# Conv0 as one pass over 108 contraction rows, with x stacked inside SBUF and relu split straight from PSUM, in an audio tower on one core

## What is computed

```python
x = jnp.pad(x, ((0, 0), (0, 0), (pad, pad)), mode='reflect')
y = jax.lax.conv_general_dilated(x, w, (stride,), 'VALID', ...) + b[None, :, None]
m = jnp.mean(y, axis=1, keepdims=True)
v = jnp.var(y, axis=1, keepdims=True, ddof=1)
h = jax.nn.relu((y - m) * jax.lax.rsqrt(v + EPS) * g[None, :, None] + b_n[None, :, None])
```

## Time and profile before

| | us |
|---|---|
| median of 3 runs | 2319.99 (2319.36 to 2320.64) |
| the profiled execution's own time | 2317.79 |
| its span, first to last instruction | 2316.0 |
| TensorE busy in the span | 2077.2 (90%) |
| VectorE, ScalarE, GpSimd busy | 1682.9, 1470.6, 777.3 |
| mean granted TensorE clock | 0.976 of full |

### The profile page before, as it was taken

The page is one execution under the profiler, slowest core; times in us unless marked ns, Lnnn a source line. Parts: engine busy times, 40 slices in busy tenths (PEclk is TensorE's granted clock), DMA queues, the critical chain, the costliest instruction groups (busy, mean ns, idle before and its releaser), DMA issues. The chain is left out here.

```text
span 2316.0 us, 35857 instructions
## 1 busy us (share of the span) xinstructions
PE 2077.2 (90%) x10589; PEld 1492.2 (64%) x10661; DVE 1682.9 (73%) x3691; ACT 1470.6 (63%) x3736; POOL 777.3 (34%) x1413
## 2 busy tenths in 40 slices
PE   4999999999999977999958888888888888877999
PEld 3788888888888865877735555555555555544554
DVE  4677787787787765566558888888888888864555
ACT  1466656666666643444438888888888888863554
POOL 0111211112112110132256555655556555534100
PEclk9999999999999998999969999999999999997999
DMA  3000000000000000000000000000000000000000
GB/s 111 11 7 7 6 10 6 6 9 6 6 9 6 0 0 1 1 1 1 1 0 1 1 1 1 1 1 1 1 1 1 1 1 1 1 1 3 12 10 14
DMA packets 14447, 15.24 MB, mean 7 GB/s; under 512 B 9995, under 2 KB 10251, under 8 KB 14051
## 3 DMA queue, kind: packets, MB, share of 16 engines
q1 hardware_dynamic: 14307, 13.58, 2.0%
HBM read 11.48 MB, written 2.10 MB: 6 GB/s over the span
## 5 line engine op out<-in xcount | busy, mean ns | idle before, releaser
L1416 ACT ACTIVATE apb<-ps,anb,arq 128x128 f32<-128x128 f32 x1024 | 455.9, 461 | 104.2 <-DVE anb L1290 103.6
L1524 POOL TENSOR_TENSOR apb<-apb,arc 128x512 f32<-128x512 f32 x256 | 266.5, 1041 | 236.5 <-DVE arc L1299 236.5
L1169 PE MATMUL ps<-akT,aqT 128*128 128x256 f32 x1024 | 263.5, 380 | 8.8 <-issue 2.5
L1284 DVE TENSOR_REDUCE amx<-ps 128x4 f32<-128x512 f32 x256 | 175.1, 684 | 97.9 <-PE ps L1169 97.3
L1180 PEld LDWEIGHTS ps<-const,apb 128*128 128x128 f32 x1024 | 112.4, 141 | 178.3 <-issue 106.5
L1416 ACT ACTIVATION_READ_ACCUMULATOR apb<-ps,anb,arq 128x1 f32 x1024 | 211.5, 207 | 0.0
L117 PE MATMUL ps<-h0h,w123h 128*128 128x512 f32 x512 | 207.2, 405 | 3.4 <-POOL h0l L602 1.7
L1169 PEld LDWEIGHTS ps<-akT,aqT 128*128 128x128 f32 x1024 | 196.3, 192 | 21.3
L1518 POOL TENSOR_TENSOR aqr<-at 128x512 f32<-128x512 f32 x128 | 163.4, 1277 | 127.1 <-DVE at L1245 127.1
L119 PE MATMUL ps<-h0h,w123l 128*128 128x512 f32 x512 | 202.8, 396 | 0.0
L1180 PE MATMUL ps<-const,apb 128*128 128x128 f32 x1024 | 162.5, 281 | 44.8 <-POOL apb L1524 43.9
(11 more groups left out here) (303 smaller groups left out, 5317.5 us busy)
## 6 DMA issues: line engine op xcount, KB each, us to landing
x<-in_x SPq DMA_DIRECT2D x32, 176.0 KB
out<-fyo SPq DMA_DIRECT2D x16, 128.0 KB, 1.9
w<-in_w SPq DMA_DIRECT2D x1, 1024.0 KB, 7.8
mw<-in_mw SPq DMA_DIRECT2D x1, 1024.0 KB, 9.6
const<-in_const SPq DMA_DIRECT2D x1, 612.0 KB
wqkv<-in_wqkv SPq DMA_DIRECT2D x1, 576.0 KB, 9.7
fw<-in_fw SPq DMA_DIRECT2D x1, 512.0 KB, 8.3
fsel<-in_fsel SPq DMA_DIRECT2D x1, 512.0 KB, 7.9
```

The lines of the kernel that those rows point to most:

```text
L1169: last = pe.matmul(bank[:, p * 2 * T:(p + 1) * 2 * T], qT[:, i % 2, 2 * k + p, :], kT[:, i // 4 % 2, i % 4, :, :].rearrange("p a s -> p (a ...
L1284: ve.tensor_reduce(mx[:, k, :], ps[:, SB[n % 3], :].rearrange("p (h s) -> p h s", h=4), AX_X, ALU.max).then_inc(S["mx"], 1)
L1416: last = ac.activation(pb[:, i % 2, head, :], ps[:, SB[n % 3], h * T:(h + 1) * T], ACT.Exp, bias=nb[:, k, h:h + 1], scale=rq[:, i % 2, hea ...
L1524: po.tensor_tensor(p, p, rc[:, i % 2, 4 * k:4 * k + 4].unsqueeze(2).to_broadcast([T, 4, T]), ALU.mult).then_inc(S["pn"], 1)
```

## The change

- Conv0's three passes become one matmul. A group now has 12 rows (10 taps, conv bias, normalization bias; the last row is left unscaled, with eps 1). Three groups make a tile of 36 rows, and a tile is stacked three times, 108 rows: x high, x low, x high, against weights high, high, low (`w0s`). The stacks `x0k` are filled for each pair by nine transfers inside SBUF, issued by SyncE, from `x0h` and `x0l`, which now have one place instead of two.
- g0 is folded into the weights, so relu needs no scale and no bias. `relu0` on ScalarE writes `h0h` directly, rounding on the way, and `low0` on VectorE computes max(psum, 0) - h0h from PSUM in one instruction of 128x1024. The cast, the tile `h0f` and the subtraction from SBUF go.
- Conv0 uses one pair of banks for both halves, so each piece waits until `low0` has read the last one (`s_h0l`).
- The wait for conv1 of the pair before stands in `relu0` now, on ScalarE (`s_y`).
- conv1 is issued in two parts. The orders of all engines are new, and all rounds are written out; no loop is left.
- Setup gains one multiplication, a load, a clear of `w0s` and nine transfers inside SBUF that fill it. The loads of x have 96 rows instead of 88.

```diff
-        h0f = sb("h0f", [128, 2, 2, T1])
+        xk = sb("x0k", [3 * SR, 2, TILES, CHUNK], F32R)
...
+                def stack(i):
+                    sp.wait_ge(s_xl, i + 1)
+                    if i == 0:
+                        sp.wait_ge(s_zero, 1)
+                    if i >= 2:
+                        sp.wait_ge(s_c0, 4 * (i - 1))
+                    for j in range(TILES):
+                        rows = slice(j * SR, min((j + 1) * SR, GR))
+                        n = rows.stop - rows.start
+                        for part, x in enumerate((xh, xl, xh)):
+                            sp.dma_start(xk[part * SR:part * SR + n, i % 2, j, :].bitcast(F32), x[rows, :].bitcast(F32)
+                                         ).then_inc(st_x[i % 2], 16)
...
                 def conv0(row, half):
...
+                        m = 4 * i + 2 * row + half
+                        if m >= 1:
+                            pe.wait_ge(s_h0l, m)
+                        if row == 0 and half == 0:
+                            pe.wait_ge(st_x[i % 2], 16 * 3 * TILES * (i // 2 + 1))
+                        for n in range(4):
+                            g = 4 * half + n
+                            last = pe.matmul(ps[:, Y0 + n // 2, (n % 2) * GC:(n % 2 + 1) * GC], w0s[:, g, :],
+                                             xk[:, i % 2, g // PER, row * GC:(row + 1) * GC], start=True, stop=True)
+                        last.then_inc(s_c0, 1)
...
-                pipeline(pe, PAIRS, [(stages[s], lag) for s, lag, _ in ORDER_CONV])
+                in_order((
+                    (conv1(0, 0), 2), (statu, 0), (conv0(0, 0), 1), (conv1(0, 1), 2), (variance("2"), 4), (statv, 0),
+                    (conv0(0, 1), 1), (conv1(1, 0), 2), (variance("1a"), 2), (conv23("3", h2h, h2l, 12, T3, s_pad2), 5),
+                    (conv0(1, 0), 1), (conv1(1, 1), 2), (variance("3"), 5), (conv23("2", h1h, h1l, 8, T2, s_pad1), 3),
+                    (conv0(1, 1), 1), (variance("1b"), 2)))
...
                 def relu0(row, half):
...
+                        ac.wait_ge(s_c0, 4 * i + 2 * row + half + 1)
+                        if i >= 1:
+                            ac.wait_ge(s_y["1" + "ab"[row]], i)
+                        ac.activation(padded(h0h, row, half), ps[:, Y0:Y0 + 2, :], ACT.Relu).then_inc(s_h0h, 1)
...
+                in_order((
+                    (rsqrt("1b"), 3), (relu("1b"), 3), (relu0(0, 0), 1), (square("1a"), 2), (rsqrt("2"), 4), (rsqrt0, 0),
+                    (relu0(0, 1), 1), (relu("2"), 4), (rsqrt("1a"), 2), (relu0(1, 0), 1), (square("3"), 5),
+                    (relu("1a"), 2), (square("1b"), 2), (rsqrt("3"), 5), (relu3, 5), (square("2"), 3),
+                    (relu0(1, 1), 1)))
...
+                def low0(row, half):
+                    def f(i):
+                        ve.wait_ge(s_h0h, 4 * i + 2 * row + half + 1)
+                        ve.scalar_tensor_tensor(out=padded(h0l, row, half), in0=ps[:, Y0:Y0 + 2, :], scalar=0.0,
+                                                in1=padded(h0h, row, half).bitcast(F32), op0=ALU.max,
+                                                op1=ALU.subtract).then_inc(s_h0l, 1)
...
+                in_order((
+                    (norm("1b"), 3), (product, 0), (split_next("1b"), 3), (low0(0, 0), 1), (split_sq("1a"), 2),
+                    (norm("2"), 4), (scaled, 0), (low0(0, 1), 1), (split_next("2"), 4), (norm("1a"), 2),
+                    (low0(1, 0), 1), (split_sq("3"), 5), (split_sq("1b"), 2), (norm("3"), 5), (split_next("1a"), 2),
+                    (split_sq("2"), 3), (low0(1, 1), 1)))
```

More of the change, by code:

```diff
@@ L34 @@
 GC = T0 // NG
+PER = 3
+TILES = -(-NG // PER)
+SR = PER * KR
 PH0 = T1 + 1
@@ L50, in offsets @@
     return out, at
[L53 to L97, removed]
[3 rows of a table removed]
-def stand_alone(ve, V):
-    ve.tensor_copy(V["carrier"][:, 1:2], V["carrier"][:, 0:1])
 def split(eng, high, low, x):
@@ L152, in audio_tower @@
         fmask = sb("fmask", [128, 2])
-        w0h, w0l = (sb(n, [GR, NG, C], F32R) for n in ("w0h", "w0l"))
+        w0s = sb("w0s", [3 * SR, NG, C], F32R)
         w123h, w123l = (sb(n, [128, 16, C], F32R) for n in ("w123h", "w123l"))
@@ L197, in _ @@
                     sp.dma_start(dst[:], A[name]).then_inc(ld_late, 16)
+                sp.wait_ge(su_v, 17)
+                sp.wait_ge(su_z, 1)
+                for j in range(TILES):
+                    rows, groups = slice(j * SR, min((j + 1) * SR, GR)), slice(j * PER, min((j + 1) * PER, NG))
+                    n = rows.stop - rows.start
+                    for part, w in enumerate((w0h, w0h, w0l)):
+                        sp.dma_start(w0s[part * SR:part * SR + n, groups, :].bitcast(F32), w[rows, groups, :].bitcast(F32)
+                                     ).then_inc(ld_w0s, 16)
+                sp.wait_ge(ld_w0s, 16 * 3 * TILES)
                 sp.wait_ge(ld_late, 15 * 16)
+            @block.gpsimd
+            def _(po):
+                po.memset(w0s[:].rearrange("p g c -> p (g c)").bitcast(F32), 0.0).then_inc(su_z, 1)
             @block.vector
@@ L338, in conv_phase, with in_order @@
         s_pad2 = sem("s_pad2")
[L340 to L345, removed]
+        def in_order(stages):
+            deepest = max(lag for _, lag in stages)
+            for n in range(PAIRS + deepest):
+                for f, lag in stages:
+                    if 0 <= n - lag < PAIRS:
+                        f(n - lag)
         with nc.Block() as block:
@@ L357, in _ @@
+                load(0)
+                load(1)
+                for i in range(PAIRS):
+                    stack(i)
+                    if i + 2 < PAIRS:
+                        load(i + 2)
             @block.tensor
             def _(pe):
[L359 to L370, removed]
@@ L372, in statv, with var_bank_free, statu @@
-                def statv(i, lo):
-                    bank_free("statv", i, lo)
+                last_var = []
+                def var_bank_free():
+                    for s, n in last_var:
+                        pe.wait_ge(s_ln[s], n)
+                    last_var.clear()
+                def statu(i):
+                    if i >= 1:
+                        pe.wait_ge(s_ln0, i)
+                    pe.wait_ge(ld_x[i % 2], 16 * (i // 2 + 1))
+                    pe.matmul(ps[0:GR, XB, :], gram[:], x8[:, i % 2, :], start=True, stop=True).then_inc(s_u, 1)
@@ L375, in statv @@
+                def statv(i):
                     pe.wait_ge(s_gx, i + 1)
-                    pe.matmul(bank["statv"][0:GR, :], K["blkones"][0:GR, 0:GR], gx[:], start=True,
-                              stop=True).then_inc(filled["statv"], 1)
+                    pe.matmul(ps[0:GR, XB, :], K["blkones"][0:GR, 0:GR], gx[:], start=True, stop=True
+                              ).then_inc(s_v, 1)
                 def conv0(row, half):
-                    stage = "conv0" + "ab"[row] + "01"[half]
@@ L382, in f @@
[L382 to L390, removed]
@@ L400, in f, with conv1 @@
+                    return f
+                def conv1(row, part):
+                    s = "1" + "ab"[row]
+                    def f(i):
+                        if part == 0:
+                            if i >= 1:
+                                pe.wait_ge(s_yn[s], i)
+                            pe.wait_ge(s_pad0[row], i + 1)
+                        for t in range(4 * part, 4 * part + 4):
                             a, q = t // 4, t % 4
                             at = q * PH0 + a
-                            last = three_passes(pe, bank[stage], w123h[:, t, :], w123l[:, t, :],
-                                                h0h[:, row, at:at + T1], h0l[:, row, at:at + T1], t == 0, t == 7)
@@ L404, in f @@
-                        last.then_inc(filled[stage], 1)
-                    return f
-                def conv23(stage, hh, hl, w_at, n_out, padded):
-                    def f(i, lo):
-                        bank_free(stage, i, lo)
+                            last = three_passes(pe, Y[s], w123h[:, t, :], w123l[:, t, :], h0h[:, row, at:at + T1],
+                                                h0l[:, row, at:at + T1], t == 0, t == 7)
+                        if part == 1:
+                            last.then_inc(s_y[s], 1)
@@ L430, in _ @@
-                stages = {"conv1a": conv1(0), "conv0a0": conv0(0, 0), "conv0a1": conv0(0, 1),
-                          "statu": statu, "conv1b": conv1(1), "var1a": var("1a"), "conv0b0": conv0(1, 0),
-                          "conv0b1": conv0(1, 1), "conv2": conv23("conv2", h1h, h1l, 8, T2, s_pad1), "statv": statv,
-                          "conv3": conv23("conv3", h2h, h2l, 12, T3, s_pad2), "var1b": var("1b"), "var2": var("2"),
-                          "var3": var("3")}
-                pipeline(pe, PAIRS, [(stages[s], lag) for s, lag, _ in ORDER_CONV])
+                        pe.matmul(ps[:, VB, 0:WIDTH[s]], onesr[:], sqh[s][:], start=True, stop=False)
@@ L489, in relu, with relu3 @@
```

(37 more changed lines are left out.)

219 lines of the change are left out of this document (104 added, 115 removed), and 3 rows, old and new, of the table ORDER_CONV.

## The result

The changed kernel takes 2369.26 us in the median of 4 runs (2367.69 to 2371.24), against 2320.31 us before (4 runs, 2319.36 to 2321.23): 1.0211 times as long, 95% interval 1.0194 to 1.0229. The prediction was 2375 us, worked out for the profiled execution; that one took 2371.24 us against 2317.79, with a span of 2369.1 us against 2316.0, 53.1 us more.

A forecast was written before the change was run, and what follows sets the result against it. TensorE was taken as the bound. A round of 27.3 us against 25.18 gave +57 over 27 rounds; with 4.2, 1.5, -8 and 2 for start and end, +57 on 2317.8, so 2375 us, range 2328 to 2412.

The forecast's parts named there:

- What goes: On TensorE 48 conv0 matmuls become 16, 3.76 us less a round.
- The first wait: TensorE stands 1.57 us before conv0's second piece, until relu and `low0` have followed the end of conv1.
- The second wait: Before conv0's third piece: TensorE is busy until 8.3 us, `low0` ends at 7.9, so no wait.
- The third wait: TensorE stands 3.6 us before the narrow `var`, as conv3's square and its split queue behind relu and `low0`.
- The round without the clock: Work 20.6 plus waits 1.6 and 3.6 give 25.8 us; as a rival (clock holds) 2333 us, chance 0.22.
- The clock: Idle before the narrow `var` lowers TensorE's clock, costing between 0 and 2.4 us a round; 1.5 taken.
- the rule quoted in the prediction: From the Trainium skill: a long enough gap, repeated in each tile of a loop, returns TensorE to half rate each time.
- The transfers: Nine stacking transfers a pair on SyncE cost nothing, with 10 us of cover; without it 6.7 us a round.
- Setup: One more load, a multiplication, nine issues at 0.43 us and a landing before the rounds: +4.2 us.
- Rounds 0 and 1: Stack, three conv0 pieces and a last of 1 us before conv1 begins, against 16.7 us: +1.5 us.
- Rounds 2 to 4: Rounds of 22.5, 20 and 20.5 us against 71.2 in all, the long wait absent in 3 and 4: -8 us.
- The end: Round 32 has the third wait too, and the drain is the same chain as before: +2 us.

The follow-up runs named there:

- e_both: Changed kernel with the split of conv3's squares moved ahead of conv0's third piece in the ScalarE and VectorE queues; 2249.65 us, 0.9703 of before.
- e_act: Changed kernel with conv3's square moved ahead of the relu of conv0's third piece on ScalarE only; 2367.17 us.
- e_dve: Changed kernel with the split of conv3's squares moved ahead of `low0` of conv0's third piece on VectorE only; 2330.67 us, 1.0051 of before.
- e_warm: Changed kernel with eight unread 512-column matmuls put into TensorE's wait before the narrow `var`; 2331.3 us, 1.0048 of before.
- e_nostack: Changed kernel with the nine stacking transfers issued for the first two pairs only, later pairs reading those stacks; 2369.36 us.
- e_relu: Changed kernel with conv0's relu given its scale and bias back as columns; 2384.06 us.
- e_conv3: Changed kernel with conv3's twelve matmuls moved ahead of conv0's second piece on TensorE; 2349.72 us, 1.0134 of before.

## Why the prediction was right

- **What goes.** Predicted 3.76 us of TensorE a round; the pieces measure 3.64. Right.
- **The first wait.** Predicted 1.57 us standing, about 1.4 as the profile counts idle time; measured 1.1. The chain had two terms too long: the relu 1.02 and not 1.20 (taking away scale and bias was costed at nothing, within 0.1, and is worth 0.18), `low0` 1.22 and not 1.30. So the new read of PSUM costs what the subtraction from SBUF cost, the floor I gave, and not the line through the smaller forms.
- **The second wait.** Predicted none, and there was none.
- **The third wait.** Predicted 3.4 us idle, once a round, for the split of conv3's squares behind two in-order queues; measured 3.2, with every link where it was said. `e_both`, `e_act` and `e_dve` show that it hangs on the order in both queues.
- **The round without the clock.** Predicted 25.8, measured 25.46; the two short terms stand once in each chain and would take 0.52 off; the round is 0.34 shorter.
- **The clock.** Predicted 1.5 us a round; measured 1.54 in a round in which it falls (27.00 less 25.46), and it fell in 22 of 26, so 1.3 on average. The kind of loss was argued from two rows of the drain; `e_warm` shows it. The size was a choice between 0 and 2.4 and not worked out, so that it came so close is luck. It also does not fall in every round, as the rule quoted in the prediction would have it. And I let it slow conv2 from its start, as after 5.58 us of idle. In this kernel the clock is as a rule still at 1.00 when the work resumes, falls within 1.5 us after that and is back 3.4 us after it fell.
- **The transfers.** Predicted nothing in the steady rounds; `e_nostack` measures nothing. The first stack took longer than I had it, 8.3 us from the end of `scaled` to conv0 (42.22 to 50.49) and not 6.7, but the cover of some 10 us was enough.
- **Setup.** Predicted 4.2, measured 5.6: the term mis-sized was the issue, some 0.77 us from one to the next and not 0.43. The nine took 6.9 us (22.91 to 29.85) and not 3.9. Part of that was made good by what came behind them: 1.65 us until the stage began where I had 2.8.
- **Rounds 0 and 1.** Predicted +1.5, measured +0.3, by an omission. conv1 did begin later, 20.3 us after `scaled` (42.22 to 62.50) against 16.7. But `statu` of round 2 now stands behind half of conv1 and not behind all of it, which I left out.
- **Rounds 2 to 4.** Predicted -8, measured -4.1. Here I was too hopeful in each round: 23.6 us against 22.5, 21.3 against 20 and 22.2 against 20.5. In round 2 the clock is at half for 6.8 us; in rounds 3 and 4 it is at full speed, and TensorE waits 2.0 and 2.4 us where I had 1.6. The remaining 0.9 us of each was not traced.
- **The end.** I had 2 us for round 32 and the drain, and 2.1 for round 31 in the 57; everything after `statu` of round 31 gives 8.9, of which some 3.6 are the excess of rounds 31 and 32. From there to the end of the stage the clock is at half for 41.0 us, against 30.7 before. `e_both` has 30.7 too and no excess there (1.4 us less than before), so the excess comes with the queue order.

The errors partly cancel, so the nearness of the total (2371 measured, 2375 predicted) is in part luck: rounds 5 to 30 gave 42 us where I had 55 (9 of the difference from the shorter chains, 4 from the clock), and all the rest gave 11 where I had 2.

## What to carry to other kernels

Before counting what a cheaper step frees on the bound engine, follow each new or moved wait to the instruction that releases it, and ask what stands behind the waiting one in its queue: here a relu that waited for a late conv1 held up a square that had long been ready. Where work must wait, put ready work ahead of it on every engine of the chain at once: on ScalarE alone it gave nothing, on VectorE alone a third, on both 120 us. And an idle stretch on TensorE can cost more than its length: here stretches of 2.4 and 3.2 us cost another 1.5 us in the rounds in which the clock fell.

## What was not expected of the hardware

The same idle stretch costs the clock in some rounds and not in others. In rounds 5 to 30 it fell in none at 1.2 us of idle (`e_warm`), in 12 of 26 at 2.4 us (`e_dve`), in 22 at 3.2 us (the changed kernel) and in 25 at 3.4 us (`e_relu`). The length alone does not decide it: `e_conv3` has 3.2 us too, and there it fell in 18. Nor is it irregular: in the changed kernel, from 394 us on, the clock falls 0.2 us after the work resumes, in the next rounds 0.5, 0.8, 1.1 and 1.4 us after it, then comes a round in which it does not fall, and the row begins again. Each fall lasts 3.4 us (6.8 in round 5). What sets this pattern was not tested.

A relu with its scale and bias given as columns takes 1.20 us on 128x1024 from PSUM, and 1.02 without. The Trainium skill, ScalarE: Activation LUTs, section "What ACT_TABLE_LOAD costs", puts about 93 ns on each such column operand; two would be 0.186 us by that, an estimate with which the 0.18 of `e_relu` agrees.

A transfer inside SBUF of up to 36 rows occupies SyncE's queue for 0.71 to 0.77 us, the load of the 96 rows of x from HBM for 0.51, in the changed kernel's trace.
